# Graph network kernel, second messages: VectorE builds the one-hot of a step in two instructions, one per tile, among its products

## What is computed

```python
w = relu(edge_feature @ W_fc1) @ W_fc2                  # 224 weights per edge
w0, w1, w2, w3, w4 = split(w, [64, 128, 160, 192])
xs, xv = s[dst], v[dst]                                  # gathered features, 64 and 32 x 3
out0a = w0 * xs
out0b = w3 * (einsum('emi,ei->em', xv, sh1) * INV_SQRT3)
out1a = (w1 * xs)[:, :, None] * sh1[:, None, :]
out1b = w2[:, :, None] * xv
out1c = w4[:, :, None] * (cross(xv, sh1[:, None, :]) * INV_SQRT2)
agg = segment_sum(concat([out0a, out0b, out1a, out1b, out1c]), src, N_NODES) / DENOM
```

## Time and profile before

| what | value |
|---|---|
| median of 3 runs | 9313.75 us (9310.38 to 9315.42) |
| profiled execution | 9304.9 us, span of its instructions 9303.1 us |
| instructions | 172881 |
| PE, DVE, ACT, POOL busy | 70%, 77%, 53%, 73% |
| granted TensorE clock, mean | 0.846 |

### The profile page before, as it was taken

The page is one execution under the profiler, slowest core; times in us unless marked ns, Lnnn a source line. Parts: engine busy times, 40 slices in busy tenths (PEclk is TensorE's granted clock), DMA queues, the critical chain, the costliest instruction groups (busy, mean ns, idle before and its releaser), DMA issues. The chain is left out here.

```text
span 9303.1 us, 172881 instructions
## 1 busy us (share of the span) xinstructions
PE 6550.8 (70%) x31164; PEld 4418.8 (47%) x31164; DVE 7166.1 (77%) x21133; ACT 4944.6 (53%) x16490; POOL 6786.3 (73%) x6877
## 2 busy tenths in 40 slices
PE   5666566664555555556555555878799999999999
PEld 3333333332222222222222222346588888888888
DVE  7666666655787887878878787854499999999995
ACT  3444444443444444444444444755477777777774
POOL 5777777777777777777777777567777777777770
PEclk7565565556888888888888888999899999999999
DMA  3222222224666666666666666656566666666667
GB/s 105 92 93 92 93 92 92 92 92 152 217 209 213 209 212 212 209 212 208 212 210 208 213 210 212 219 182 198 168 170 169 168 170 170 168 169 168 171 165 229
DMA packets 1190048, 1591.50 MB, mean 171 GB/s; under 512 B 452553, under 2 KB 967369, under 8 KB 1189577
## 3 DMA queue, kind: packets, MB, share of 16 engines
q1 hardware_dynamic: 790264, 838.69, 29.1%
q0 software_dynamic: 328704, 651.74, 24.2%
q10 hardware_dynamic: 70992, 100.14, 3.0%
HBM read 1000.68 MB, written 1051.46 MB: 221 GB/s over the span
## 5 line engine op out<-in xcount | busy, mean ns | idle before, releaser
L1705 PE MATMUL pair<-prod_m,hot_m 128*128 128x160 f32 x14848 | 2244.8, 304 | 154.7 <-DVE prod_m L1914 118.5
L1587 POOL DMA_INDIRECT feat_m<-feat_tab,rows_m x1856 | 1819.3, 980 | 579.4 <-issue 428.5
L1705 PEld LDWEIGHTS pair<-prod_m,hot_m 128*128 128x128 f32 x14848 | 2043.2, 190 | 356.2 <-issue 355.2
L1737 ACT ACTIVATE prod_m<-part_m,rows_m 128x64 f32<-128x64 f32 x5568 | 1432.3, 337 | 1387.6 <-DVE part_m L1934 1184.0
L1725 ACT ACTIVATE hot_m<-hot_m,rows_m 128x128 f32<-128x128 f32 x5568 | 1728.5, 389 | 688.4 <-DVE hot_m L1897 680.2
L1598 POOL DMA_INDIRECT fetched_m<-feat_tab,index_m x1664 | 1696.5, 1020 | 516.2 <-issue 492.7
L718 POOL DMA_INDIRECT sorted_rows<-rows_e,place_e x1664 | 1612.1, 969 | 541.2 <-issue 504.9
L1686 PE MATMUL bank<-prod_m,hot_m 128*128 128x449 f32 x2476 | 1166.9, 597 | 843.6 <-DVE prod_m L1954 426.4
L1615 POOL DMA_INDIRECT sorted_rows<-later_m,place_m x1248 | 1251.2, 1003 | 464.5 <-issue 375.7
L1914 DVE TENSOR_TENSOR prod_m<-rows_m,feat_m 128x192 f32<-128x192 f32 (+2 forms) x4640 | 1284.5, 309 | 0.0
L1686 PEld LDWEIGHTS bank<-prod_m,hot_m 128*128 128x128 f32 x2476 | 446.6, 201 | 1463.1 <-issue 1161.0
(11 more groups left out here) (251 smaller groups left out, 10147.3 us busy)
## 6 DMA issues: line engine op xcount, KB each, us to landing
agg_tab<-acc_m ACTq DMA_DIRECT2D x928, 320.0 KB
rows_m<-sorted_rows SPq DMA_DIRECT2D x928, 229.0 KB
agg_tab<-acc_m ACTq DMA_DIRECT2D x928, 224.5 KB
rows_m<-sorted_rows SPq DMA_DIRECT2D x928, 197.0 KB
feat_m<-feat_sorted SPq DMA_DIRECT2D x928, 160.0 KB
feat_sorted<-fetched_m SPq DMA_DIRECT2D x208, 640.0 KB
turned_m<-in_turned ACTq DMA_DIRECT2D x159, 256.0 KB
agg_s<-agg_tab SPq DMA_DIRECT2D x98, 320.0 KB, 4.0
```

The costliest lines, as they stand in the source:

```text
L1587: pool.indirect_dma_start(out=feat[s % RING][:, k, :], out_offset=None, in_=g.feat_tab[l.n], in_offset=bass.IndirectOffsetOnAxis(ap=rows[s ...
L1705: mm = pe.matmul(dst, hot[s % l.hot_bufs][:, k, q, :], rhs, start=(k == 0 and q < 2), stop=(k == ST_TILES - 1), skip_group_check=True)
L1737: ins = act.activation(prod[s % prods][:, k, at:at + S0], part[s % 2][:, k, 0:S0], ACT.Copy, scale=rows[s % HELD][:, k, l.sh_at + m:l.sh_a ...
```

## The change

For L1 the single one-hot instruction over both tiles is replaced by `tile_hot`, called for k = 0 and k = 1: a tensor_scalar over 128 columns of one tile, with base node and key as two operands of one value per partition. The waits stand before k = 0, the signal `hot_ready` comes after k = 1. The products are split into three pairs: the two `scalars` between the one-hots, `vectors(128)` with `vectors(160, ..., 2, 3)` after the second one-hot, then the sum, then `vectors(192)` with `vectors(160, ..., 0, 2)`, which now gives `prod_ready`. L0 keeps its order.

```diff
+            def tile_hot(step, it, s, k):
+                u = it * TURN + s
+                if k == 0:
+                    dve.wait_ge(rows_here[s % HELD], 16 * (use(it, s, HELD) + 1))
+                    if step is None or step >= l.hot_bufs:
+                        dve.wait_ge(sum_ready, u - l.hot_bufs + 1)
+                        dve.wait_ge(hot_scaled, u - l.hot_bufs + 1)
+                ins = dve.tensor_scalar(
+                    hot[s % l.hot_bufs][:, k, 0, :], iota, g.base_node[:, bass.ds(u, 1)],
+                    rows[s % HELD][:, k, l.key_at:l.key_at + 1].bitcast(F32), ALU.add, ALU.is_equal)
+                if k == ST_TILES - 1:
+                    ins.then_inc(hot_ready, 1)
+
...
                 else:
-                    at = l.hot0[0]
-                    scalars(0, at, 1)
+                    scalars(0, l.hot0[0], 1)
                     scalars(64, l.pieces_at + 64, 2)
-                    vectors(128, at + 64, 0, 3, 1)
+
+            def middle_products(step, it, s):
+                _, _, _, vectors = forms(s)
+                vectors(128, l.hot0[0] + 64, 0, 3, 1)
+                vectors(160, l.pieces_at + 32, 2, 3, 1)
...
                     vectors(192, p0, 0, 3, 3)
-                    vectors(160, p0 + 160, 0, 2, 3)
-                    vectors(160, p0 + 32, 2, 3, 1).then_inc(prod_ready, 1)
+                    vectors(160, p0 + 160, 0, 2, 3).then_inc(prod_ready, 1)
...
             def step_(step, it, s):
-                if sends:
-                    rank(step, it, s)
+                if not sends:
+                    stage(1, lambda *a: tile_hot(*a, 0))(step, it, s)
+                    stage(2, first_products)(step, it, s)
+                    stage(1, lambda *a: tile_hot(*a, 1))(step, it, s)
+                    stage(2, middle_products)(step, it, s)
+                    stage(l.add_lag, add_up)(step, it, s)
+                    stage(2, other_products)(step, it, s)
+                    return
+                rank(step, it, s)
                 prepare(step, it, s)
                 stage(1, one_hots)(step, it, s)
                 stage(2, first_products)(step, it, s)
```

## The result

| what | before | after |
|---|---|---|
| median of 5 runs | 9311.73 us | 9447.75 us (9442.26 to 9479.04) |
| profiled execution | 9304.9 us, span 9303.1 | 9442.26 us, span 9440.5 |
| ratio to before | 1 | 1.0153 (95% interval 1.0141 to 1.0166) |

What follows compares the result with a forecast made beforehand. POOL was taken to bound the second messages at 2.570 us a step, DVE next. The one-hot pair's 259 ns makes DVE's step 2.722: plus 142 us, 9447 for a profiled execution, 9455 forecast, range 9340 to 9500.

Steps and rivals of the forecast that it cites:

- The bound: Second messages: POOL's two gathers set the pace at 2.570 us a step; DVE second at 2.463, so 0.107 us free.
- DVE takes over: Second messages after the change: DVE's step of 2.722 us exceeds POOL's 2.570, so DVE sets the pace.
- The pair: DVE's two tensor_scalars, 408 ns each, 327 start to start: 654 ns for the old one-hot's 395, plus 259 a step.
- the one-operand rival: One operand's load is hidden or only one of two costs: pair 520 ns, step 2.588 us, 9352 us; chance 0.10.
- The moved products at 0: DVE's six products keep columns and operands, two only change place: cost 0.
- ACT's cover of 2.3 us: ACT's scaling, begun later, is done near 3.1 us; PE needs it 2.3 us later, so the delay is hidden.
- The sum: 927 steps of 2.722 us plus 7 for the start: 2530 us against 2388, plus 142; 9455 on the runs' footing.
- The waits for features: DVE's waits for gathered features in the second messages fall from 91.7 us to under 15, ending save at the start.
- my signs of being wrong: Tensor_scalar of 340 ns or less, DVE still waiting for features, or its instructions apart with idle time put to issue.
- Faster, from POOL: Rival: the change ends long gathers caused by DVE's products; POOL's step 2.50 us, 63 us less, 9251; chance 0.03.
- The rule of the Trainium skill: A DVE instruction with two SBUF inputs contends with a GpSimd instruction that reads SBUF; no size given.
- POOL would show gaps over 0.3 us: POOL, with slower consumers, fills its six buffers, then waits for DVE's products in gaps longer than 0.3 us.

## Why the prediction was right, and where it was not

The bound. POOL at 2.570 a step and DVE second at 2.463 was read rightly: the change was free up to 0.107 us a step and paid beyond, 0.245 - 0.107 each of 927 times, 128 us. The run with the pair in the old order measured just that. The other 20 of the changed kernel's 148 are in the main DVE's waits for features behind long gathers, 17 us. Right as well was that DVE takes over.

The pair. Forecast 654 ns, measured 644, from 408 ns an instruction against 394. The row of one column with two operands carried: the sum of base, operands and columns holds to 4%. The difference is in part in the profile's ends, as all of DVE's durations read some 9 ns shorter in this execution (862 for 871, 272 for 281). The run with the pair alone shows that this term is 128 of the stage's 148 us, and the runs with fewer operands that its parts are the ones named. A slip without effect: in the one-operand rival the old one-hot's fixed part, 475 - 264, is 211 ns and not 207.

The moved products at 0: shown by the order-only run, 1.0003, for the single one-hot; beside the pair the new order has the long gathers. ACT's cover of 2.3 us held: in the timeline of the changed kernel PE starts 0.25 us behind the last product each step, as before. The profile puts 189.2 us of PE's waits to ACT's one-hots. But what ACT ends near PE's start is the scaling for the step after, and PE doesn't need it: at 7522.42 us PE starts while ACT's last instruction still runs, to 7522.49.

The sum. Plus 142 for the stage, measured 148; 9447 for a profiled execution, measured 9442; 9455 against a median of 9447.75. That the totals agree to 5 and 7 us is in part luck. The pair was put 13 us too dear (2.722 for 2.708, 927 times), some 20 us of long gathers were not foreseen, and the stages around the second messages took 11 us less in this execution, for no cause in the change.

The waits for features: under 15 us were forecast, 24.2 came, 7 of them at the start. That DVE still waits for features was one of my signs of being wrong. The others follow 17 gathers of 2.4 us, each of which takes DVE's whole step, where two gathers usually fit. They come in five bunches of three or four, 270 to 620 us apart. Here is the first of them, and the end of the third group of products after its start:

```profile
7345.95 2.40 POOL L1587 DMA_INDIRECT feat_m<-feat_tab,rows_m  x1 [0.30 <-issue]
...
7347.06 0.47 DVE L1927 TENSOR_TENSOR prod_m<-rows_m,feat_m 128x192 f32<-128x192 f32 x2
```

It starts inside the group that ends at 7346.09 and ends at 7348.35, 0.82 us after the group that ends at 7347.53, so it was not let through in the two gaps of 0.25 us between, where only a one-hot stands. Another 173 gathers start at the same place of DVE's step, within 20 ns, and last 0.95 to 0.98 us. Why just these 17 are held is open.

**The step that failed** is in the rival "Faster, from POOL". I set the contention aside because "the usual gather is 0.94 to 0.95 whatever DVE does beside it". The usual one is, as it starts where DVE reads no two SBUF tensors or just gets past them, but the row of 1.62 us stood beside it in the same group, and I did not lay it on DVE's timeline. The contention is real and costs the kernel before 0.7%. It didn't decide here, because DVE's step went to 2.71 and covers gathers of 1.15 us. The rule of the Trainium skill that I quoted there (SBUF — State Buffer, "Who interferes with whom") is borne out: with one SBUF tensor instead of two in each product, the long gathers are gone. Its weight in the forecast was small, as the rival asked for a pair of at most 432 ns and the pair costs 644. For the same reason my forecast that POOL would show gaps over 0.3 us was wrong: it is held inside the gathers, and the gaps appear only once the products read PSUM.

## What to carry to other kernels

Price a short DVE instruction by its operands as well as its columns, from the narrowest row that has the same operands: here some 60 ns for each per-partition one, so one wide scalar_tensor_tensor over two tiles (395 ns) beats two tensor_scalars (644). Before counting an engine's slack as free, lay the rare long instructions of its neighbour on its own timeline; if they end at one fixed place of its step, the two contend. And where two engines run periods that differ by a per cent or two, the faster one may gain by being made a little slower than the other.

## What the runs showed of the hardware

A gather of POOL lasts 0.946 us undisturbed. One that starts inside a group of DVE products with two SBUF tensors, or at most 0.07 us ahead of it, can be held. It then ends 0.82 us after a product, mostly the group's last (245 gathers over 0.98 us in the kernel before, the longest 1.64). One that starts over 0.1 us ahead of the group is not held there (1000 gathers, none over 0.98 us); in the changed kernel 4 of 715 such gathers were. Products that read PSUM and one SBUF tensor don't do this (1856 gathers, none over 0.98 us).

With such products and DVE's step above POOL's 2.50 us the two lock: nearly every gather pair takes DVE's step, and the excess lies in the gathers' durations, where the profile names no wait for it. With DVE's step 37 ns below it, they slip past each other, and each meeting costs up to 0.7 us. From 2.463 to 2.51 us of DVE work a step the kernel gets faster by 0.6%, from there on slower.

A tensor_scalar of 128 fp32 columns lasted 394 ns out of PSUM and 332 out of SBUF with the same operands; the second also met the gathers more often (37 of 2.25 us or more), and 16 gathers end 0.82 us after such an instruction. With one and with no per-partition operand it lasted 334 and 278 ns out of PSUM.
